# Last attention of a four-block network: second scores and value sums moved to the head of a step, next batch's preparation begun four steps sooner, first batch's preparation split over the engines

## The chip, the cores and the metric

One core of a Trainium2 chip runs the whole program. The metric is device time in microseconds (us) from start to end of one execution. The kernel before took 2774.77 us, the median of three executions (2765.41, 2774.77 and 2776.35).

Engines are named as the profile names them: PE is TensorE (PEld its weight loads), DVE is VectorE, ACT is ScalarE, POOL is GpSimd, SP issues DMAs. Each engine executes its own instructions in program order and waits on semaphores for the others.

## The reference

The network applies four blocks to `x` of shape (4, 512, 256): `x = x + layernorm(block(layernorm(x)))`. The blocks are a windowed attention, an attention with a mixture of experts, the attention changed here, and a second mixture of experts. The block that the change touches is:

```python
def _L1_attn_ref(x, ln_q_g, ln_q_b, Wq, bq, ln_kv_g, ln_kv_b, Wkv, bkv, ln_h_g, ln_h_b, Wo, bo):
    q = (layernorm(x, ln_q_g, ln_q_b) @ Wq + bq)      # 16 heads of 16
    kv = (layernorm(x, ln_kv_g, ln_kv_b) @ Wkv + bkv)
    ...
    q = apply_rotary(q, x)          # tables scaled by the norm of the row of x
    k = apply_rotary(k, x)
    qn = layernorm(q, ln_h_g, ln_h_b)                 # over each head's 16 values
    kn = layernorm(k, ln_h_g, ln_h_b)
    logits = jnp.einsum('bhqd,bhkd->bhqk', qn, kn) / jnp.sqrt(jnp.float32(HD))
    att = jax.nn.softmax(logits, axis=-1)
    a = jnp.einsum('bhqk,bhkd->bhqd', att, v)
    a = a.transpose(0, 2, 1, 3).reshape(b, c, d)
    return a @ Wo + bo
```

There are 4 batches of 512 rows. A batch is 4 tiles of 128 rows and has 16 heads, which is 8 pairs of heads.

## The kernel before

The stage is the function `attention2`. It is one software pipeline over steps `s`, and every engine runs the same loop over `s` with its own list of operations in each step. A batch has 32 steps: 4 groups of 8 steps, a group being two pairs of heads times four row tiles. Batch `b` has its scores in steps 32b to 32b+31. Below, `i` is the step within a batch, and "step 3 of a group" is `s % 8 == 3`.

Scores are computed twice. The first scores (`scores`, L1835, two matmuls into a pair of PSUM banks of `c_first`) serve only to find each row's maximum: `maximum` (L2080) on DVE. `c_first` has two such pairs, used in turn by everything that goes through it (list `pairs`), so that each use waits for the reader of the use before last. At the end of a group, `max_high` (L1972, ACT) and `max_low` (L2086, DVE) put the maxima into spare columns of the stacked q. The q of the group is turned again (`turn_q("again")`, L1821 on PE, copied by `copy_q`, L1966, on ACT). 14 steps after the first scores (`SECOND`) come the second scores, transposed (`scores_t`, L1848, two matmuls into the two banks of `c_second`). Then follow `exps` (L1980, two ACT operations), and two steps after that (`LAG`), once per two steps, the value sums (`values`, L1860, eight matmuls). Both banks of `c_second` are written in each step, so that `scores_t` of a step waits for both exponentials of the step before:

```python
if g >= 1:
    pe.wait_ge(s_ex, 2 * g)
```

In a step, PE's order before the change is: turn q again (step 3 of a group), first scores, turn q first (step 4; the q of the next group), turn keys, project, turn the outputs of a group (`turn_o`), the transposes `turn_a` and the output projection `out` of the batch before, then `scores_t`, and then `values` in odd steps. ACT's order is: `max_high` (step 0), copy q again (step 3), `exps`, copy q first, `copy_keys`, `root`, `high`, `copy_a`. DVE's is: `maximum`, `max_low` (step 1), `copy_o` (step 7), tables, `read_qk`, `cos_products`, `head_sums`, `centre`, `square_sums`, `inverse`, `read_v`, `divide`, `add_bias`. The function has no DMA in its loop.

The preparation of a batch runs during the scores of the batch before it; for batch 0 it runs ahead, in steps -32 to -1. For each of four tiles it is: `project("qk")` (L1802, PE), `read_qk` (L2033), `cos_products` (L2053) on DVE and `sin_products` (L2183) on POOL, `rotate` (L2189, POOL), `head_sums` (L2058), `centre` (L2063), `square` (L2194, POOL), `square_sums` (L2069), then for all four tiles together `root` (L1938, ACT) and `inverse` (L2075, DVE), then per tile `scale` (L2199), two `gains` (L2207) on POOL, `high` (L1950, four ACT copies), `low` (L2214, two POOL operations), `turn_keys` (L1812, PE) and `copy_keys` (L1959, ACT). `project("v")` has its own four steps, and its DVE reader is `read_v` (L2040). All projections, `turn_o`, `turn_a` and `out` share one bank (`c_x`, list `singles`), and each waits for the reader of the use before it. The steps come from `tile_at(s, first, apart)`: qk in i = 0, 3, 6, 9, v in 16 to 19, `root` and `inverse` in 17, `scale` in 18, 20, 22, 24, `high` in 20 to 26, `low` in 21 to 27, `turn_keys` and `copy_keys` in 23, 25, 27, 29.

## Time and profile before

| | us |
|---|---|
| median of three executions | 2774.77 |
| the profiled execution | 2782.3 |
| its span, first to last instruction | 2780.3 |
| the stage changed here, first projection to last bias | 1936 to 2364.6 |
| of it, preparation of batch 0 | 51.7 |
| of it, scores of the four batches and the tail | 377 |

The profile's page shows PE busy for 84% of the span, DVE for 59%, ACT for 46% and POOL for 49%, and a mean granted TensorE clock of 0.923 of full speed. The page's averages cover stages with different limits, so the changed stage is read alone. The tables by stretch give each engine's busy time between two points of time. The timeline gives single operations in order, with the idle time before each in brackets and what ended it.

### The profile page before, as it was taken

Reading aid. Unit: us, or ns where it says so; the run is one execution under the profiler, and the core shown is the slowest. Engines: PE = TensorE matmul, PEld = TensorE weight load, DVE = VectorE, ACT = ScalarE, POOL = GpSimd, SP = SyncE. Lnnn points to the kernel's source line nnn. Section 1 sums busy time; section 2 is a strip of 40 time slices with the busy share of each in tenths; the row PEclk is TensorE's granted clock in tenths of the full one; section 3 lists DMA queues with packets and bytes.
Section 4 is the critical chain, followed back from the end, with each engine's and each line's share of the span. In section 5 each row is a group of like instructions: output and inputs, shape, how many; then the busy total and the mean of one; then the engine's idle time right before and its main releaser. Section 6 shows DMA issues by size and latency. Waiting matters only on the chain. (4 is left out here: it accounts for less than half of the span.)

```text
span 2780.3 us, 41037 instructions
## 1 busy us (share of the span) xinstructions
PE 2342.3 (84%) x12100; PEld 1559.3 (56%) x12100; DVE 1649.0 (59%) x5313; ACT 1274.5 (46%) x3678; POOL 1358.1 (49%) x1301
## 2 busy tenths in 40 slices
PE   6999999994899999999998499963577887599991
PEld 5888888882455555555554456531333343466661
DVE  7667676665766766766774533327566753653334
ACT  3444444443556656656666244421166564143331
POOL 2444454441555555555554178862634310138885
PEclk9999999997899999999999599985799998699996
DMA  5000000002000000000001545550000000515554
GB/s 167 16 15 1 15 15 15 16 4 87 1 1 1 1 1 1 1 1 1 1 1 32 219 81 87 86 117 23 0 1 1 1 1 1 198 35 86 87 85 112
DMA packets 72818, 112.26 MB, mean 40 GB/s; under 512 B 11504, under 2 KB 59632, under 8 KB 72240
## 3 DMA queue, kind: packets, MB, share of 16 engines
q0 software_dynamic: 30336, 42.73, 9.3%
q1 hardware_dynamic: 38080, 63.15, 6.5%
q10 hardware_dynamic: 4224, 4.19, 0.4%
q8 instruction: 88, 1.44, 0.2%
q14 instruction: 90, 0.74, 0.1%
HBM read 80.69 MB, written 36.32 MB: 42 GB/s over the span
## 5 line engine op out<-in xcount | busy, mean ns | idle before, releaser
L1059 POOL TENSOR_TENSOR b_sm<-b_sm,b_rden 128x128 f32<-128x128 f32 (+3 forms) x512 | 355.7, 722 | 357.4 <-DVE b_rden L1012 357.4
L952 ACT ACTIVATE b_sm<-b_sm,b_mn 128x128 f32<-128x128 f32 (+3 forms) x512 | 285.1, 569 | 23.0 <-DVE b_mn L1004 22.0
L943 ACT ACTIVATE b_pt<-b_t 128x128 f32<-128x128 f32 (+3 forms) x512 | 196.1, 440 | 144.9 <-PE b_t L883 144.5
L1004 DVE CUSTOM_DVE_ANT_0 b_sm<-b_f,maskB 128x128 f32<-128x128 f32 (+3 forms) x512 | 233.5, 489 | 3.3 <-issue 2.2
L873 PE MATMUL b_f<-b_k,b_q 64*128 64x128 f32 (+3 forms) x1024 | 209.9, 486 | 29.1 <-DVE b_prod L993 14.7
L993 DVE SCALAR_TENSOR_TENSOR b_prod<-b_f,b_sin 32x512 f32<-32x512 f32 x320 | 219.9, 687 | 4.3
L1428 POOL DMA_INDIRECT XN<-rows,m_slots x158 | 158.1, 1001 | 94.0 <-issue 47.5
L2080 DVE TENSOR_REDUCE c_nm<-c_first 128x2 f32<-128x1024 f32 x128 | 155.1, 1219 | 82.2 <-PE c_first L1835 82.2
L1980 ACT ACTIVATE c_pt<-c_second 128x512 f32<-128x512 f32 x256 | 139.2, 598 | 123.8 <-PE c_second L1848 123.6
L883 PE MATMUL b_t<-ident,b_sm 128*128 128x128 f32 x1280 | 194.6, 283 | 0.9 <-ACT b_pt L943 0.8
L409 POOL TENSOR_TENSOR a_q<-a_prod 128x512 f32<-128x512 f32 x64 | 81.8, 1278 | 228.8 <-DVE a_prod L355 228.8
L883 PEld LDWEIGHTS b_t<-ident,b_sm 128*128 128x128 f32 x1280 | 143.4, 141 | 87.4 <-issue 60.5
L860 PE MATMUL b_f<-HT,b_w 128*128 128x512 f32 x320 | 154.6, 607 | 0.0
L897 PE MATMUL b_t<-b_pt,Y 128*64 128x512 f32 (+3 forms) x1024 | 151.9, 439 | 2.5 <-ACT b_pt L943 2.5
L1247 PE MATMUL m_p<-WM,Y 128*128 x316 | 151.5, 602 | 2.8 <-issue 2.8
L323 ACT ACTIVATE a_s<-a_s,a_nmx 128x192 f32<-128x192 f32 (+1 forms) x256 | 110.1, 431 | 87.6 <-DVE a_nmx L368 87.6
L1435 POOL DMA_INDIRECT acc<-Y,m_slots x79 | 125.4, 1587 | 32.0 <-issue 21.1
L1435 POOL DMA_INDIRECT acc<-m_plain,m_slots x79 | 125.4, 1588 | 30.8 <-issue 20.2
L908 PE MATMUL b_y<-b_wo,b_ot 128*128 128x256 f32 x512 | 134.9, 387 | 0.0
L897 PEld LDWEIGHTS b_t<-b_pt,Y 128*64 128x64 f32 x1024 | 68.4, 136 | 117.2 <-issue 78.1
L637 POOL TENSOR_TENSOR X<-X,Y 128x1024 f32<-128x1024 f32 x16 | 38.9, 2430 | 184.2 <-DVE Y L565 184.2
L873 PEld LDWEIGHTS b_f<-b_k,b_q 64*128 64x128 f32 x1024 | 79.0, 187 | 86.9 <-issue 62.3
(283 smaller groups left out, 5393.4 us busy)
## 6 DMA issues: line engine op xcount, KB each, us to landing
WM<-in_m_w_dram SPq DMA_DIRECT2D x4, 3072.0 KB, 17.5
WM<-in_m_w_dram SPq DMA_DIRECT2D x4, 2432.0 KB, 14.0
acc<-in_zeros_dram SPq DMA_DIRECT2D x3, 2176.0 KB, 16.2
n_part<-acc SPq DMA_DIRECT2D x12, 512.0 KB, 7.8
a_wa<-in_a_wa_dram SPq DMA_DIRECT2D x8, 512.0 KB, 4.5
b_w<-in_b_w_dram SPq DMA_DIRECT2D x1, 3072.0 KB, 9.9
XN<-rows,m_slots POOLq DMA_INDIRECT x158, 2.8
X<-in_x_dram SPq DMA_DIRECT2D x4, 512.0 KB, 5.7
```

What stands on the lines that cost most here:

```text
L860: x = pe.matmul(bank[:, :], w[:, k, pair, j, :], c.HT[:, k, b * SEQ:(b + 1) * SEQ], start=first, stop=last)
L873: pe.matmul(front_bank(("s", S, head))[:, 0:keys(t)], q_r[r, M % 3, t * P:(t + 1) * P], k_r[r, pg % 2, 0:keys(t)], start=True, stop=True). ...
L883: x = pe.transpose(bank[:, k * P:(k + 1) * P], sm[:, slot(S, head), k * P:(k + 1) * P], c.ident[:, :])
L897: x = pe.matmul(bank[r:r + B_HD, k * P:SEQ], v_s[:, b % 2, k, pair * P + r:pair * P + r + B_HD], pt[:, M % 2, head, k, k * P:SEQ], start=( ...
L943: act.activation(pt[:, M % 2, head, 0:t + 1, t * P:(t + 1) * P], back_bank(("t", S, head))[:, 0:keys(t)].rearrange("p (k n) -> p k n", n=P ...
L952: act.activation(sm[:, s, 0:keys(t)], sm[:, s, 0:keys(t)], ACT.Exp, scale=-1.0, bias=mn[:, s:s + 1], accum_out=den[:, s:s + 1]).then_inc(s ...
L993: x = dve.scalar_tensor_tensor(to[dst, 1, :], bank[src, :], scale, sin[src, :], ALU.mult, ALU.mult)
L1004: dve.tensor_tensor_reduce(sm[:, s, 0:keys(t)], front_bank(("s", S, head))[:, 0:keys(t)], mask[:, SEQ - keys(t):SEQ], 1.0, -3 * NEG, ALU.a ...
L1059: pool.tensor_tensor(sm[:, s, 0:keys(t)], sm[:, s, 0:keys(t)], rden[:, s:s + 1].to_broadcast([P, keys(t)]), ALU.mult).then_inc(s_pn, 1)
L1428: pool.indirect_dma_start(out=xg[:, b % RING, :], out_offset=None, in_=rows_dram[:, :], in_offset=IOA(ap=slots[:, b:b + 1], axis=0)).then_ ...
L1435: pool.indirect_dma_start(out=acc_dram[b % 2][:, :], out_offset=IOA(ap=slots[:, b:b + 1], axis=0), in_=ys[:, b % 4, :], in_offset=None, co ...
L2080: dve.tensor_reduce(nm[:, t, 2 * j:2 * j + 2], two_banks(("max", f)), AX.X, ALU.max, negate=True).then_inc(s_nm, 1)
```

## The change

It does four things, all in `attention2`.

1. In PE's loop, `scores_t` and `values` move from the end of a step to its head, ahead of "turn q again" and of the first scores. DVE's and ACT's orders are not changed by this.
2. The preparation of batches 1 to 3 starts four steps sooner: qk in i = -4, -1, 2, 5 (28 and 31 of the batch before that), products one step and rotate two steps after each, `root` in 13, `inverse` in 14, `scale` in 14 to 20, `low` in 18 to 24, keys in 20, 22, 24, 26, v in 18 to 21. `high` is split into `high_q` (two copies) and `high_k` (two copies, a step later), with a semaphore each.
3. "Turn q first" moves from step 4 to step 5 of a group, `turn_o` and `divide` from 29 to 25 steps after the group's first step, `turn_a` from 55 and 56 to 54 and 55. The loop has 2 steps fewer at its end and 4 more at its start.
4. Batch 0's preparation gets its own schedule (`EARLY`). `root` and `inverse` run for one tile at a time, so that `scale` begins in i = 5 and not 18. `sin_products` and `scale` go from POOL to DVE, `square` from POOL to ACT. Keys are turned in i = 10, 13, 16, 19.

```diff
@@ -1677,19 +1677,22 @@
     NP = PER_BATCH * BATCH
     TURN, SECOND, LAG = 3, 14, 2
     QUADS = 2
-    FIRST_STEP, LAST_STEP = -PER_BATCH, NP - PER_BATCH + 62
+    FIRST_STEP, LAST_STEP = -PER_BATCH - 4, NP - PER_BATCH + 60

     def turned_again(s):
         return s // GROUP - 1 if s % GROUP == TURN and 0 <= s // GROUP - 1 < GROUPS_ALL else None

     def turned_first(s):
-        return s // GROUP + 1 if s % GROUP == 4 and 0 <= s // GROUP + 1 < GROUPS_ALL else None
-
-    def tile_at(s, first, apart):
-
-        b, i = s // PER_BATCH + 1, s % PER_BATCH - first
-        t = i // apart
-        return b * TB + t if b < BATCH and i % apart == 0 and 0 <= t < TB else None
+        return s // GROUP + 1 if s % GROUP == 5 and 0 <= s // GROUP + 1 < GROUPS_ALL else None
+
+    def tile_at(s, what):
+
+        for b in range(BATCH):
+            first, apart = (EARLY if b == 0 else LATER)[what]
+            i = s - PER_BATCH * (b - 1) - first
+            if i >= 0 and i % apart == 0 and i // apart < TB:
+                return b * TB + i // apart
+        return None

...

-    KEYS_AT, PROJ_AT, V_AT, O_AT, A_AT, OUT_AT = 23, 0, 16, 29, 55, 58
+    O_AT, A_AT, OUT_AT = 25, 54, 58
+    LATER = {"qk": (-4, 3), "products": (-3, 3), "rotate": (-2, 3), "sums": (0, 3), "centre": (1, 3), "square": (2, 3),
+             "square_sums": (3, 3), "scale": (14, 2), "shift": (15, 2), "high_q": (16, 2), "high_k": (17, 2), "low": (18, 2),
+             "keys": (20, 2), "v": (18, 1)}
+    EARLY = {**LATER, "scale": (5, 3), "shift": (6, 3), "high_q": (7, 3), "high_k": (7, 3), "low": (8, 3), "keys": (10, 3)}
...
                 def turn_keys(n):
-                    pe.wait_ge(s_hi, n + 1)
+                    pe.wait_ge(s_hik, n + 1)
                     pe.wait_ge(s_lo, n + 1)
                     pair_free(("keys", n))
                     to = two_banks(("keys", n))
...
                 for s in range(FIRST_STEP, LAST_STEP):
+                    g, m = s - SECOND, s - SECOND - LAG
+                    if 0 <= g < NP:
+                        scores_t(g)
+                    if 0 <= m < NP and m % 2 == 1:
+                        values(m // 2)
                     if turned_again(s) is not None:
                         pe.wait_ge(s_nl, turned_again(s) + 1)
                         turn_q("again", turned_again(s), s_tr2)
...
                     if turned_first(s) is not None:
                         grp = turned_first(s)
                         if grp % 4 == 0:
-                            pe.wait_ge(s_hi, grp + 4)
+                            pe.wait_ge(s_hiq, grp + 4)
                             pe.wait_ge(s_lo, grp + 4)
                             if grp >= 8:
                                 pe.wait_ge(s_clear, grp // 4 - 1)
                         turn_q("first", grp, s_trq)
-                    if tile_at(s, KEYS_AT, 2) is not None:
-                        turn_keys(tile_at(s, KEYS_AT, 2))
-                    if tile_at(s, PROJ_AT, 3) is not None:
-                        project("qk", tile_at(s, PROJ_AT, 3))
-                    if tile_at(s, V_AT, 1) is not None:
-                        project("v", tile_at(s, V_AT, 1))
+                    if tile_at(s, "keys") is not None:
+                        turn_keys(tile_at(s, "keys"))
+                    if tile_at(s, "qk") is not None:
+                        project("qk", tile_at(s, "qk"))
+                    if tile_at(s, "v") is not None:
+                        project("v", tile_at(s, "v"))
                     if group_at(s, O_AT) is not None:
                         turn_o(group_at(s, O_AT))
...
-                    g = s - SECOND
-                    if 0 <= g < NP:
-                        scores_t(g)
-                    m = g - LAG
-                    if 0 <= m < NP and m % 2 == 1:
-                        values(m // 2)
...
+                def root(n, tiles):
+
+                    act.wait_ge(s_ssq, n + tiles)
+                    at = slice(n % TB, n % TB + tiles)
+                    act.activation(std[:, at, :], ssq[:, at, :], ACT.Sqrt, bias=c.eps[:, :], scale=1.0 / C_HD).then_inc(s_std, 1)
+
+                def square(n):
+                    act.wait_ge(s_cen, n + 1)
+                    act.wait_ge(s_ssq, n)
+                    act.activation(sq[:, :], qk[:, n % TB, :], ACT.Square).then_inc(s_sq, 1)
+
+                def high_q(n):
                     b, t = n // TB, n % TB
+                    act.wait_ge(s_n, n + 1)
+                    if b >= 2 and t == 0:
+                        act.wait_ge(s_tr2, (b - 1) * 4)
+                    for place in (0, 1):
+                        x = act.activation(stack_q[b % 2][:, t, :, place * C_HD:(place + 1) * C_HD].bitcast(F32R),
+                                           heads(qk[:, t, 0:DIM]), ACT.Copy)
+                    x.then_inc(s_hiq, 1)
+
+                def high_k(n):
                     act.wait_ge(s_n, n + 1)
                     if n >= 2:
                         act.wait_ge(s_trk, n - 1)
-                    if b >= 2 and t == 0:
...
+                    for place in (0, 2):
+                        x = act.activation(stack_k[:, n % 2, :, place * C_HD:(place + 1) * C_HD].bitcast(F32R),
+                                           heads(qk[:, n % TB, DIM:W2]), ACT.Copy)
+                    x.then_inc(s_hik, 1)
...
-                    if tile_at(s, KEYS_AT, 2) is not None:
-                        copy_keys(tile_at(s, KEYS_AT, 2))
-                    if i == 17 and b < BATCH:
-                        root(b)
-                    if tile_at(s, 20, 2) is not None:
-                        high(tile_at(s, 20, 2))
+                    if tile_at(s, "keys") is not None:
+                        copy_keys(tile_at(s, "keys"))
+                    if i == 13 and 0 < b < BATCH:
+                        root(b * TB, TB)
+                    if tile_at(s, "square") is not None and tile_at(s, "square") < TB:
+                        square(tile_at(s, "square"))
+                    if tile_at(s, "square_sums") is not None and tile_at(s, "square_sums") < TB:
+                        root(tile_at(s, "square_sums"), 1)
+                    if tile_at(s, "high_q") is not None:
+                        high_q(tile_at(s, "high_q"))
+                    if tile_at(s, "high_k") is not None:
+                        high_k(tile_at(s, "high_k"))
...
+                def inverse(n, tiles):
+
+                    b, at = n // TB, slice(n % TB, n % TB + tiles)
+                    dve.wait_ge(s_std, n + 1 if b == 0 else TB + b)
                     if b > 0:
                         dve.wait_ge(s_scaled, b * TB)
-                    dve.reciprocal(rstd[:, :, :], std[:, :, :]).then_inc(s_rs, 1)
+                    dve.reciprocal(rstd[:, at, :], std[:, at, :]).then_inc(s_rs, 1)
...
+                def scale(n):
+                    dve.wait_ge(s_rs, n + 1)
...
+                def sin_products(n):
+                    dve.wait_ge(s_r, n)
...
-                    if i == 0 and b < BATCH:
-                        tables_of(b)
-                    if tile_at(s, PROJ_AT, 3) is not None:
-                        read_qk(tile_at(s, PROJ_AT, 3))
-                    if tile_at(s, 1, 3) is not None:
-                        cos_products(tile_at(s, 1, 3))
-                    if tile_at(s, 4, 3) is not None:
-                        head_sums(tile_at(s, 4, 3))
-                    if tile_at(s, 5, 3) is not None:
-                        centre(tile_at(s, 5, 3))
-                    if tile_at(s, 7, 3) is not None:
-                        square_sums(tile_at(s, 7, 3))
-                    if i == 17 and b < BATCH:
-                        inverse(b)
-                    if tile_at(s, V_AT, 1) is not None:
-                        read_v(tile_at(s, V_AT, 1))
+                    if i == PER_BATCH - 4 and b + 1 < BATCH:
+                        tables_of(b + 1)
+                    if tile_at(s, "qk") is not None:
+                        read_qk(tile_at(s, "qk"))
+                    if tile_at(s, "products") is not None:
+                        cos_products(tile_at(s, "products"))
+                        if tile_at(s, "products") < TB:
+                            sin_products(tile_at(s, "products"))
+                    if tile_at(s, "sums") is not None:
+                        head_sums(tile_at(s, "sums"))
+                    if tile_at(s, "centre") is not None:
+                        centre(tile_at(s, "centre"))
+                    if tile_at(s, "square_sums") is not None:
+                        square_sums(tile_at(s, "square_sums"))
+                    if i == 14 and 0 < b < BATCH:
+                        inverse(b * TB, TB)
+                    if tile_at(s, "scale") is not None and tile_at(s, "scale") < TB:
+                        inverse(tile_at(s, "scale"), 1)
+                        scale(tile_at(s, "scale"))
+                    if tile_at(s, "v") is not None:
+                        read_v(tile_at(s, "v"))
...
-                    pool.wait_ge(s_rs, n // TB + 1)
+                    pool.wait_ge(s_rs, TB + n // TB)
...
+                    pool.wait_ge(s_hiq, n + 1)
+                    pool.wait_ge(s_hik, n + 1)
...
+                    if tile_at(s, "products") is not None and tile_at(s, "products") >= TB:
+                        sin_products(tile_at(s, "products"))
+                    if tile_at(s, "rotate") is not None:
+                        rotate(tile_at(s, "rotate"))
+                    if tile_at(s, "square") is not None and tile_at(s, "square") >= TB:
+                        square(tile_at(s, "square"))
+                    if tile_at(s, "scale") is not None:
+                        if tile_at(s, "scale") >= TB:
+                            scale(tile_at(s, "scale"))
+                        gains(tile_at(s, "scale"), 0)
+                    if tile_at(s, "shift") is not None:
+                        gains(tile_at(s, "shift"), 1)
+                    if tile_at(s, "low") is not None:
+                        low(tile_at(s, "low"))
```

## Rows read from the trace of the kernel before

**Rows 1.** Busy us (x instructions) by stretch: PE, PEld, DVE, ACT, POOL; PEclk; DMA share.
```profile
1936.00:1987.70 51.70, 27.57 (x74) 15.17 (x74) 20.17 (x33) 10.75 (x22) 36.46 (x36) 0.60 0.00 0
1987.70:2019.10 31.40, 21.17 (x76) 9.79 (x76) 29.43 (x41) 5.67 (x7) 13.92 (x15) 0.84 0.00 1
2019.10:2067.20 48.10, 36.53 (x206) 18.43 (x206) 25.47 (x30) 32.35 (x61) 20.96 (x21) 0.93 0.00 1
2161.50:2254.70 93.20, 74.88 (x424) 36.17 (x424) 60.85 (x84) 54.73 (x102) 34.94 (x36) 0.98 0.00 1
2254.70:2317.80 63.10, 55.39 (x352) 25.08 (x352) 43.93 (x50) 41.21 (x76) 0.00 (x0) 1.00 0.00 1
2317.80:2345.60 27.80, 20.18 (x103) 6.35 (x102) 4.13 (x8) 17.07 (x32) 0.00 (x0) 0.78 0.00 1
```

**Rows 2.** Timeline: start, us, engine, line, [idle before]; steps 96 to 104, no preparation.
```profile
2256.15 0.51 PE L1835 MATMUL c_first<-c_kt,c_qt 64*128 64x512 f32 x2
...
2258.51 1.06 PE L1860 MATMUL c_pv<-c_pt,c_v 128*32 128x512 f32 x8
...
2259.84 0.42 PE L1848 MATMUL c_second<-c_qt,c_kt 64*128 64x512 f32 x2
...
2260.19 1.10 PE L1821 MATMUL c_first<-ident,XN 128*128 128x128 f32 x8
2260.30 1.08 ACT L1980 ACTIVATE c_pt<-c_second 128x512 f32<-128x512 f32 x2 [0.59 <-PE c_second L1848]
...
2261.32 0.51 PE L1835 MATMUL c_first<-c_kt,c_qt 64*128 64x512 f32 x2
2261.32 1.03 ACT L1966 ACTIVATE c_qt<-c_first 128x1024 fp32r<-128x1024 f32 x1
...
2261.87 1.22 DVE L2080 TENSOR_REDUCE c_nm<-c_first 128x2 f32<-128x1024 f32 x1 [0.60 <-PE c_first L1835]
...
2262.24 1.08 ACT L1980 ACTIVATE c_pt<-c_second 128x512 f32<-128x512 f32 x2
...
2271.20 0.51 PE L1835 MATMUL c_first<-c_kt,c_qt 64*128 64x512 f32 x2
2271.29 0.23 ACT L1972 ACTIVATE c_stack_q<-c_nm 128x16 fp32r<-128x16 f32 x1
```

**Rows 3.** Timeline, PE: first scores of steps 64, 72 and 88 (batch 2).
```profile
2163.03 0.50 PE L1835 MATMUL c_first<-c_kt,c_qt 64*128 64x512 f32 x2
...
2184.60 0.49 PE L1835 MATMUL c_first<-c_kt,c_qt 64*128 64x512 f32 x2
...
2227.32 0.49 PE L1835 MATMUL c_first<-c_kt,c_qt 64*128 64x512 f32 x2
```

**Rows 4.** PE's groups in batch 2 (busy, mean ns, idle before); a table load on ACT.
```profile
L1802 PE MATMUL c_x<-c_wqkv,HT 128*128 128x512 f32 (+1 forms) x32 | 12.5, 512 | 4.1 <-DVE c_v L2040 3.6 <-DVE c_a_t L2108 0.5
...
L1812 PE MATMUL c_first<-ident,c_stack_k 128*128 128x128 f32 x32 | 5.2, 315 | 3.9 <-ACT c_qt L1966 3.9
...
2210.71 1.28 ACT L1980 ACT_TABLE_LOAD   x1
```

**Rows 5.** Timeline of batch 0's preparation.
```profile
1945.94 0.69 DVE L2063 SCALAR_TENSOR_TENSOR c_qk<-c_hsum,c_qk 128x512 f32<-128x512 f32 x1
...
1951.02 1.44 DVE L2063 SCALAR_TENSOR_TENSOR c_qk<-c_hsum,c_qk 128x512 f32<-128x512 f32 x1
...
1964.26 2.61 POOL L2207 TENSOR_TENSOR c_qk<-c_qk,c_gq 128x512 f32<-128x512 f32 x2
1964.54 2.08 PE L1802 MATMUL c_x<-c_wqkv,HT 128*128 128x256 f32 x4 [0.52 <-DVE c_v L2040]
...
1967.54 0.71 ACT L1950 ACTIVATE c_stack_k<-c_qk 128x256 fp32r<-128x256 f32 x2
...
1982.19 1.94 PE L1812 MATMUL c_first<-ident,c_stack_k 128*128 128x128 f32 x8 [3.09 <-ACT c_stack_k L1950]
...
1982.85 0.73 POOL L2214 TENSOR_TENSOR c_stack_k<-c_qk,c_stack_k 128x256 fp32r<-128x256 f32 x1
```

More of the change, by code:

```diff
@@ L1708, in attention2 @@
             pairs.append(("first", turned_first(s)))
-        if tile_at(s, KEYS_AT, 2) is not None:
-            pairs.append(("keys", tile_at(s, KEYS_AT, 2)))
-        if tile_at(s, PROJ_AT, 3) is not None:
-            singles.append(("qk", tile_at(s, PROJ_AT, 3)))
-        if tile_at(s, V_AT, 1) is not None:
-            singles.append(("v", tile_at(s, V_AT, 1)))
+        if tile_at(s, "keys") is not None:
+            pairs.append(("keys", tile_at(s, "keys")))
+        if tile_at(s, "qk") is not None:
+            singles.append(("qk", tile_at(s, "qk")))
+        if tile_at(s, "v") is not None:
+            singles.append(("v", tile_at(s, "v")))
         if group_at(s, O_AT) is not None:
@@ L1761, in attention2 @@
         s_sq, s_ssq, s_std, s_rs = sem("square"), sem("square_sum"), sem("std"), sem("rstd")
-        s_scaled, s_p, s_n, s_hi, s_lo = sem("scaled"), sem("times_gain"), sem("normed"), sem("high"), sem("low")
+        s_scaled, s_p, s_n, s_lo = sem("scaled"), sem("times_gain"), sem("normed"), sem("low")
+        s_hiq, s_hik = sem("high_q"), sem("high_k")
         s_trk, s_ke, s_trq, s_qe = sem("keys_turned"), sem("keys_copied"), sem("q_turned"), sem("q_copied")
```

40 lines of the change are left out of this document (11 added, 29 removed).

## The prediction

> **What bounds the kernel now.** I read the page for its own time first: the profiled execution took 2782.3 us, 2.0 more than its span and 7.5 more than the median of 2774.8, so I work out a difference on the trace and add it to the median. Only `attention2` changes, and no DMA moves in it [rows 1]. The table by stretch shows four regimes. In batch 0's preparation (51.7 us) POOL is busy for 36.5 us and PE idles at a granted clock of 0.60. From the first scores to step 15 (31.4 us) DVE is full: 29.4 busy. In batch 2, as in batch 1, PE is busy for 74.9 of 93.2 us, and no engine is full. In batch 3, without preparation, a group of 8 steps takes 15.05 us (first scores at 2256.15 and 2271.20 [rows 2]), and PE's 55.4 of 63.1 us is not what holds it. The timeline shows what does: a loop through PE and ACT. The exponentials take 1.08 us, the next second scores wait for both of them, and the exponentials after that start about 0.46 us after their matmuls do (2259.84 and 2260.30), so that a step takes at least 1.08 + 0.46 and some 0.1 for the handing over, 1.7 us [rows 2].
>
> **The head of the step.** PE's order repeats from step to step, so moving `scores_t` (T) and `values` (V) to the head only rotates it: T comes one place earlier against the first scores (S), and V lies ahead of "turn q again" (A) and not behind it. What counts is what lies between the end of one pair of exponentials and the start of the next. Durations: T and S hold PE for 0.43 each, V 1.0, A or "turn q first" (F) 1.02, a copy of q 1.03 and an exponential pair 1.08 [rows 2].
> - Step 3 (A). Before, A runs during the exponentials of step 2, and T runs during A's copy, which is why the pairs at 2260.30 and 2262.24 are 1.94 apart although a copy lies between them [rows 2]. ACT's order still has the copy ahead of the exponentials. After, A stands behind T and V, and T behind the exponentials of step 2: 1.08 + 0.06 + 0.43 + 1.0 + 1.02 + 0.11 + 1.03 = 4.7 us apart, 2.8 more.
> - Step 0. `max_high` is ahead of `exps` on ACT and waits for the maximum of step 7. S now follows V: 1.42 for T and V, 0.55 to DVE, 1.22 for the maximum, 0.3 for the copy, so the exponentials of step 0 start 3.5 us after T of step 7 and 3.0 after its exponentials, not 1.7: 1.3 more. Before, `max_high` at 2271.29 waited for nothing [rows 2].
> - Steps 4 and 5 (F). F at step 5 lies after T, V and S, with its copy ahead of the next exponentials: 3.5 us. At step 4 it made one interval of about 2.7 and one of 1.9; now the others are 1.7. Together 0.3 more or less, taken as 0.
> - `turn_o` (0.6) moves into an odd step, beside V: T + V + S + 0.6 = 2.45 against 1.7, 0.8 more.
>
> A group without preparation goes from eight intervals of 15.05 to 3.0 + 1.7 + 2.45 + 4.7 + 1.7 + 1.7 + 3.5 + 1.7 = 20.4. The same addition for the order before gives 15.6, 0.5 too much, so I take +5.0 for a group. Batch 3 has four: +20, less 2.4 since the two output projections there no longer lie beside V and A on PE: +17.5. The tail has one step 0, one step 3 and one `turn_o` more, at a clock of 0.78 [rows 1]: +4.5.
>
> **Batches 1 and 2.** Here PE is 80% busy, and the waits above are filled with preparation. I added up a batch in the same way, group by group, from 19.6 us (20.4 less the walk's 4% excess): group 1 with projections in steps 2 and 5 and one left over from step 31, +4.5 = 24.1; group 2 with ACT's root, 1.28 + 0.4 + 1.28, +3 = 22.6; group 3 with v and keys, +3.3 = 22.9; group 4 with keys, one output projection beside nothing else, and the next projection, +4.2 = 23.8; in all 93.4. Before, the first group took 21.6, the next two 42.7 and the last 28.8, which is 93.1 (first scores at 2163.03, 2184.60, 2227.32 and 2256.15 [rows 2, 3]). So the gain is where the keys were: 28.8 becomes about 24, because keys no longer share steps 27 and 29 with A and F. PE waited 3.9 us a batch for a copy of q ahead of `turn_keys`, and 3.6 for `read_v`, which was queued on DVE behind `inverse` [rows 4]. It is given back in groups 1 and 2 through steps 0 and 3. I take +0.5 for each batch, +1 in all. The bounds are -7.5 (those two PE waits gone, nothing given back) and +7.
>
> **Batch 0's scores.** Steps 0 to 15 are DVE's [rows 1]. Two of batch 1's tiles are read and one is multiplied before step 0, and T of a step now precedes S of that step: -2.3. ACT loads a table once where it did three times between step 14 and step 18, as the roots of batch 1 now come before the first exponentials: two loads of 1.28 and a stall behind them [rows 4]. With the quieter group of keys this makes 43.1 for the 48.1 us [rows 1]: -5.0.
>
> By the Trainium skill (ScalarE: Activation LUTs, "What ACT_TABLE_LOAD costs") a switch of tables costs about 2.66 us with a drain, not the load of 1.28 alone. By it, batch 0 would gain some 2.8 us more; no row shows a drain.
>
> **Batch 0's preparation.** Splitting root and inverse lets `scale` of tile 0 finish at about 1954, nine us sooner than before. From there POOL has two gains (2.6) and two `low` (1.45) a tile [rows 5]. But there is a loop: in i = 10, 13 and 16 ACT copies the keys of a tile first and does `high` of the next tile behind that, so `high` waits for `turn_keys` of the tile before. One turn of that loop is low 1.45, `turn_keys` 1.94 at the low clock, copy 1.03, high 1.43, and 0.25 of handing over: 6.1 us a tile, against 5.05 of POOL alone before. From `low(0)` at 1962.5 three turns end `low(3)` at 1980.8, where it was 1983.6 [rows 5]. Then PE still has, in order, keys 3 (1.94), v of tiles 1 to 3 (2.08 each at the low clock [rows 5], 1.13 at the high one, plus 0.5 for `read_v`), the projection of tile 4 (1.98), F (1.1) and the projection of tile 5 (1.98) ahead of the first scores: 11 to 14 us. Before, it was 4.1. The first scores come at 1990 to 1994.5 where they came at 1987.7: I take +4.5, with bounds of -1.5 (all at the high clock, POOL's pace) and +7.
>
> **The sum.** +4.5 - 2.3 - 5.0 + 1 + 17.5 + 4.5 = +20.2. On the median: 2774.8 + 20.2 = 2795.
>
> **The rivals.**
> 1. The waits of steps 0 and 3 cost little, since ACT has slack (41.2 busy of 63.1 in batch 3 [rows 1]), and the earlier preparation gives what it can: -7.5 in each of batches 1 and 2, -7.3 in batch 0, -1.5 in the preparation, 0 in batch 3: -24, 2751. Against it: ACT's slack is idle time inside the loop and not beside it [rows 2]. Chance 0.1.
> 2. Both hold by half: batch 3 and the tail +11, batches 1 and 2 together -5, batch 0 -7, the preparation +2: +1, 2776. Chance 0.3.
> 3. Slower than forecast: with PE idling longer in batch 3, its granted clock falls as in the tail (0.78 against 1.00 [rows 1]). This decides if PE's busy share of 0.88 there falls to the tail's 0.73; my sum gives 55.4 of 80.6, 0.69. T, V, A and S of batch 3 then take up to twice their time: in the loop that is 8 x 0.1, A and V 2.0, F 1.0 and so on, about 4 a group: +36, 2811. Chance 0.15.
> 4. DVE and POOL hold each other up in batch 0's preparation. `centre` took 1.44 us at one place, beside POOL's `rotate`, and 0.69 at another [rows 5]. If all two-input operations of tiles 2 and 3 on DVE are stretched so, (0.75 + 1.1 + 0.7) x 2, the first scores come 5 us later still: 2800. Chance 0.05.
>
> The Trainium skill (SBUF — State Buffer, "SBUF: two separate sides") calls the port pair that DVE and GpSimd share an exclusive lock, whose loser waits for the whole instruction; by that rule rival 4 holds, and moving work from POOL to DVE gains nothing there.
>
> **How the numbers follow.** The forecast case has 0.4 by itself, between 2785 and 2805. The range that should hold 8 in 10 takes in rivals 2 to 4 and the bounds of the preparation and of the middle batches: 2768 to 2818; rival 1 and a worse clock are left out. A difference of 0.5%, 14 us, is about what a measurement of this kernel can tell from none. Faster by that is rival 1 with a little of rival 2: 0.12. Within it is most of rival 2 and the low end of the forecast: 0.30. Slower is the rest: 0.58.
>
> **What would show each step.** In the profile after: exponentials 4.7 us apart around A in batch 3, with ACT idle until `c_first` L1821; ACT idle before `max_high`, released by DVE `c_nm`; a period of about 20 us a group in batch 3 at PE busy of 0.7; the waits of `turn_keys` on `c_qt` gone and the fourth group of batches 1 and 2 near 24; two table loads fewer on ACT in batch 0; the first scores 54 to 58 us after the first projection. I am wrong if batch 3 still takes 63 us, or if PE's V and A fit into the exponentials' shadow.

## The result

The changed kernel takes 2840.22 us (median of 4, 2830.73 to 2847.46) against 2772.21 for the kernel before: a ratio of 1.0236, 95% interval 1.0207 to 1.0265. That is +68 us where +20.2 was forecast, and outside the range. The profiled execution took 2844.9 us, its span is 2843.1.

Between the two profiled executions (2782.3 and 2844.9 us) the stage went from 427.7 to 493.0 us, counted from the first projection to the end of the last output projection, and the rest of the program was 2.7 shorter. I cut the stage at the second scores of steps 15, 31, 63, 95 and 127, which are the same work in every kernel of this study, and use these stretches throughout, as the rest of the program varies by several us from run to run. Each row of stretches comes from one execution.

| stretch | before | after | measured | forecast |
|---|---|---|---|---|
| preparation of batch 0 | 51.5 | 57.1 | +5.5 | +4.5 |
| first scores to step 15 | 31.4 | 36.3 | +4.9 | -2.3 |
| 15 to 31 | 48.1 | 45.6 | -2.5 | -5.0 |
| batch 1, 31 to 63 | 94.4 | 104.7 | +10.3 | +0.5 |
| batch 2, 63 to 95 | 93.1 | 103.2 | +10.1 | +0.5 |
| batch 3, 95 to 127 | 64.0 | 89.3 | +25.3 | +17.5 |
| tail, 127 to the end | 45.1 | 56.7 | +11.6 | +4.5 |

The table by stretch of the kernel after (columns as in [rows 1]) has the same stretches; the last line ends at step 141.

```profile
1937.20:1994.30 57.10, 29.50 (x80) 15.71 (x80) 27.88 (x53) 13.59 (x29) 23.48 (x22) 0.67 0.00 0
1994.30:2030.60 36.30, 19.26 (x65) 9.96 (x64) 30.91 (x38) 5.96 (x8) 14.16 (x16) 0.72 0.00 0
2030.60:2076.20 45.60, 39.52 (x208) 18.91 (x208) 24.52 (x31) 29.95 (x58) 21.93 (x23) 0.85 0.00 1
2076.20:2181.00 104.80, 83.44 (x426) 39.06 (x426) 61.57 (x84) 55.11 (x101) 34.92 (x37) 0.85 0.00 1
2181.00:2284.20 103.20, 81.22 (x420) 37.70 (x420) 59.35 (x77) 55.10 (x101) 32.32 (x34) 0.85 0.00 1
2284.20:2373.60 89.40, 65.91 (x354) 28.75 (x354) 44.07 (x50) 42.64 (x77) 0.00 (x0) 0.85 0.00 0
2373.60:2411.00 37.40, 25.96 (x102) 8.20 (x102) 4.82 (x9) 16.22 (x30) 0.00 (x0) 0.57 0.00 1
```

DVE and ACT are busy in batches 1 to 3 for what they were before. PE is busy for 81.2 us in batch 2 where [rows 1] has 74.9, and for 65.9 in batch 3 where it had 55.4, though it executes the same matmuls: the granted clock is 0.85 of full speed in all three batches, where it was 0.96, 0.98 and 1.00. The forecast had reckoned with the waits alone.

The waits are there, as forecast. The timeline of batch 3 after, a group at the full clock:

```profile
2334.21 0.23 ACT L1992 ACTIVATE c_stack_q<-c_nm 128x16 fp32r<-128x16 f32 x1 [1.60 <-DVE c_nm L2122]
2334.33 1.07 ACT L2000 ACTIVATE c_pt<-c_second 128x512 f32<-128x512 f32 x2
...
2335.45 0.50 PE L1856 MATMUL c_second<-c_qt,c_kt 64*128 64x512 f32 x2 [2.06 <-ACT c_pt L2000]
...
2338.44 1.08 ACT L2000 ACTIVATE c_pt<-c_second 128x512 f32<-128x512 f32 x2 [1.36 <-PE c_second L1856]
...
2341.01 1.09 PE L1829 MATMUL c_first<-ident,c_stack_q 128*128 128x128 f32 x8
...
2342.14 1.02 ACT L1986 ACTIVATE c_qt<-c_first 128x1024 fp32r<-128x1024 f32 x1 [2.61 <-PE c_first L1829]
...
2343.06 1.08 ACT L2000 ACTIVATE c_pt<-c_second 128x512 f32<-128x512 f32 x2
...
2344.19 0.50 PE L1856 MATMUL c_second<-c_qt,c_kt 64*128 64x512 f32 x2 [1.66 <-ACT c_pt L2000]
```

`max_high` waits 1.60 us for the maximum of step 7, and the exponentials of step 0 stand behind it. "Turn q again" (A) stands behind T and V, its copy waits 2.61, and the exponentials at 2338.44 and 2343.06 are 4.62 apart (4.7 forecast, 1.94 before [rows 2]). PE idles 2.06 and 1.66 us for them. One turn from A to A is 19.94 us here (20.4 forecast). But the turn before it, with the same operations, is 24.62 long. The table by stretch, from A to A:

```profile
2296.45:2321.07 24.62, 18.06 (x88) 7.56 (x85) 10.89 (x12) 10.62 (x19) 0.00 (x0) 0.71 0.00 1
2321.07:2341.01 19.94, 13.04 (x89) 5.53 (x85) 10.89 (x12) 10.62 (x19) 0.00 (x0) 1.00 0.00 0
```

DVE and ACT do the same to a hundredth; PE takes 5.0 us more and the turn 4.7. So in this turn nearly all that PE loses at the low clock is lost to the whole.

### The profile page after: what moved, and what is told of

The parts are those of the page before. It is cut to its first block and busy times, and to the rows that moved or that the text cites. A ratio compares the mean times of both kernels' runs of the same rounds, so it can differ in the third digit from the quotient of the medians.

```text
span 2843.1 us, 41054 instructions
## 1 busy us (share of the span) xinstructions
PE 2372.7 (83%) x12100; PEld 1569.2 (55%) x12100; DVE 1658.3 (58%) x5328; ACT 1276.5 (45%) x3683; POOL 1343.9 (47%) x1285
## 5 line engine op out<-in xcount | busy, mean ns | idle before, releaser
L952 ACT ACTIVATE b_sm<-b_sm,b_mn 128x128 f32<-128x128 f32 (+3 forms) x512 | 285.0, 569 | 22.9 <-DVE b_mn L1004 22.0
L1856 PE MATMUL c_second<-c_qt,c_kt 64*128 64x512 f32 x256 | 74.1, 575 | 81.4 <-ACT c_pt L2000 81.2
## 6 DMA issues: line engine op xcount, KB each, us to landing
WM<-in_m_w_dram SPq DMA_DIRECT2D x4, 3072.0 KB, 17.5
```

Source lines behind the costliest of these rows:

```text
L952: act.activation(sm[:, s, 0:keys(t)], sm[:, s, 0:keys(t)], ACT.Exp, scale=-1.0, bias=mn[:, s:s + 1], accum_out=den[:, s:s + 1]).then_inc(s ...
```

## The experiments

Times in us; stretches as above, the last two columns the tail and the whole stage. The ratio is to the kernel before on the same chip, with its 95% interval. The kernel before had medians of 2776.9 to 2780.8 on the chips of the experiments, so kernels of different rows are compared by the ratio or by the stage and not by the median alone.

| kernel | median | ratio | prep. | to 15 | to 31 | b. 1 | b. 2 | b. 3 | tail | stage |
|---|---|---|---|---|---|---|---|---|---|---|
| before | 2772.2 | 1 | 51.5 | 31.4 | 48.1 | 94.4 | 93.1 | 64.0 | 45.1 | 427.7 |
| after | 2840.2 | 1.0236 [1.0207, 1.0265] | 57.1 | 36.3 | 45.6 | 104.7 | 103.2 | 89.3 | 56.7 | 493.0 |
| e1_head_only | 2787.2 | 1.0043 [1.0017, 1.0068] | 51.5 | 31.4 | 45.3 | 90.9 | 87.8 | 80.0 | 43.9 | 430.8 |
| e2_no_head | 2789.1 | 1.0052 [1.0032, 1.0072] | 54.7 | 36.0 | 48.2 | 101.0 | 99.8 | 63.6 | 42.1 | 445.4 |
| e3_again_first | 2783.0 | 1.0025 [0.9999, 1.0051] | 54.7 | 36.0 | 42.5 | 94.7 | 94.5 | 75.6 | 39.8 | 437.7 |
| e4_scores_twice | 2829.9 | 1.0207 [1.0156, 1.0257] | 54.6 | 36.0 | 43.3 | 105.2 | 102.2 | 89.0 | 47.7 | 478.0 |
| e5_again_tv_scores | 2766.7 | 0.9945 [0.9926, 0.9964] | 52.3 | 31.4 | 45.5 | 86.1 | 85.9 | 73.3 | 43.9 | 418.3 |
| e6_max_high_late | 2753.0 | 0.9900 [0.9878, 0.9921] | 52.4 | 30.9 | 43.8 | 84.7 | 83.3 | 67.6 | 39.4 | 402.1 |
| e7_high_ahead | 2823.0 | 1.0156 [1.0125, 1.0186] | 51.8 | 37.1 | 44.4 | 102.9 | 103.5 | 90.5 | 47.7 | 477.8 |
| e8_early_only | 2781.7 | 1.0002 [0.9985, 1.0020] | 54.1 | 31.4 | 54.3 | 94.8 | 95.8 | 64.1 | 39.0 | 433.5 |
| e9_both_orders | 2780.4 | 1.0008 [0.9986, 1.0029] | 54.7 | 36.0 | 42.3 | 91.0 | 88.5 | 70.0 | 41.3 | 423.9 |
| e10_first_in_4 | 2766.9 | 0.9972 [0.9947, 0.9998] | 57.2 | 34.7 | 41.6 | 89.6 | 88.7 | 68.0 | 41.4 | 421.2 |
| e11_both_high_ahead | 2774.7 | 0.9994 [0.9974, 1.0013] | 51.8 | 37.1 | 41.9 | 89.6 | 88.5 | 70.0 | 41.4 | 420.3 |
| e12_late_early | 2743.8 | 0.9886 [0.9860, 0.9912] | 48.4 | 31.4 | 42.4 | 85.6 | 83.3 | 67.5 | 41.2 | 399.8 |
| e13_filled | 2814.9 | 1.0145 [1.0105, 1.0185] | 57.3 | 36.0 | 45.6 | 101.2 | 98.2 | 82.4 | 47.5 | 468.0 |
| e14_again_filled | 2791.9 | 1.0054 [1.0027, 1.0081] | 54.7 | 36.0 | 42.5 | 96.3 | 95.1 | 75.3 | 41.5 | 441.3 |

The preparation of one and the same code took 54.7 or 57.1 us, at a granted clock of 0.72 or 0.67: a difference of 2.5 us there says nothing about a kernel.

**The two halves of the change.** e1 is the kernel before with only the head:

```diff
                 for s in range(FIRST_STEP, LAST_STEP):
+                    g, m = s - SECOND, s - SECOND - LAG
+                    if 0 <= g < NP:
+                        scores_t(g)
+                    if 0 <= m < NP and m % 2 == 1:
+                        values(m // 2)
                     if turned_again(s) is not None:
...
-                    g = s - SECOND
-                    ...
```

> The kernel before with the second scores and value sums at the head of a step, and nothing else changed. Theory W (the order at the head makes new waits on ACT at steps 0 and 3 of a group, and the idle PE then loses its clock): 3.0 + 1.7 + 1.85 + 4.7 + 1.7 + 2.5 + 2.45 + 1.7 = 19.6 us for a group of batch 3 at the high clock instead of 15.05, up to 25 with part of it at the low one; in all +40 to +60 us on the 2772 of before, 2812 to 2832. Theory P (the moved preparation and batch 0's own schedule cost most of the 68 us): at most +20, under 2795, and batch 3 near 64 us.

e2 is the kernel after with these lines back at the end of the step.

> The changed kernel with the second scores and value sums back at the end of a step, and the rest of the change kept. Theory W: batch 3 back near 64 us and a clock near 1.00 from step 32 to 127, batches 1 and 2 at 93 or a little under, the preparation of batch 0 still 5 us longer: 2765 to 2782. Theory P: the loss stays, over 2815.

Both missed, and in the same way: batch 3 came as expected (e1 80.0, e2 63.6), the middle batches did not. The head alone makes them 3.5 and 5.3 us shorter, the rest of the change alone 6.6 and 6.7 longer, the two together 10.3 and 10.1 longer. Over the stage e1 adds 3.1 us and e2 17.7, and both together 65.3: 44.5 us belong to neither half alone, but to the two meeting.

**One swap.** e3 is the kernel after with A ahead of T and V at the head of the step, so that A runs during the exponentials before it.

```diff
                 for s in range(FIRST_STEP, LAST_STEP):
+                    if turned_again(s) is not None:
+                        pe.wait_ge(s_nl, turned_again(s) + 1)
+                        turn_q("again", turned_again(s), s_tr2)
                     g, m = s - SECOND, s - SECOND - LAG
```

> The changed kernel with one swap: in step 3 of a group, turning q again is put ahead of the second scores and value sums. Theory W: the pairs of exponentials around it are about 2 us apart and not 4.7, so 2.7 us less in each of 16 groups, 43 us, and some of the clock's loss besides: 2785 to 2797. The wait of max_high in step 0 stays. If the clock were lost for another reason, under 15 us would come back: over 2825.

The median fell by 57 us (ratio 1.0236 to 1.0025), the stage by 55.3: more than the 44.5 that neither half explains. The same swap on the old preparation (e5 below against e1) takes 12.5 off the stage. So A's place behind T and V costs 12.5 us there and 55.3 with the moved preparation, and this difference of 42.8 is nearly all of the 44.5.

**The clock.** e4 repeats the first scores of even steps.

```diff
-                    for half in range(2):
+                    for half in (0, 1) * (2 - f % 2):
```

> The changed kernel with each pair of first-score matmuls of an even step executed twice into the same banks (64 pairs more, 0.43 us each, 27 us of work for PE that computes nothing new). Theory W says that the part of the loss beyond the walk is the granted clock, which falls where PE idles: with PE busier the clock from step 31 to 127 rises from 0.85 to 0.95 or more, and the time falls by 5 to 20 us, to 2820 to 2835. If the clock is not what PE's idle time costs, the added work leaves the time equal or makes it 5 to 27 us longer.

The time came as expected, the clock did not: it stayed near 0.85 in batches 1 to 3, these kept their length, and the gain of 15.0 us in the stage lies ahead of and behind them. With the clock unmoved, the lower time does not bear out the theory. The copies were spread evenly, not where PE waits. e13 puts them there, from batch 1 on:

```diff
-                    for half in range(2):
+                    for half in (0, 1) * (1 + ((4, 0, 2, 3, 1, 0, 2, 0)[f % GROUP] if f >= PER_BATCH else 0)):
```

> The changed kernel with copies of the first scores of the same step (same values into the same banks, which do no useful work) from batch 1 on: four more in step 0 of a group, two in step 2, three in step 3, one in step 4, two in step 6, each just ahead of a place where PE waits for the exponentials (2.06, 0.95, 1.66, 0.82 and some 1.3 us in batch 3): 0.4 us each, 4.8 us a group, so that PE works through those waits and still comes to its second scores in time. No wait and no order is changed. Theory K (the low granted clock after these waits costs the time: within the changed kernel the same work between two "turn q again" took 24.6 us with low stretches and 19.9 without): the granted clock of batch 3 goes from 0.85 to 0.97 or more, batch 3 takes 79 to 83 us and not 89.3, the middle batches 94 to 99 and not 104.7 and 103.2, the steps from 127 to 141 some 34 and not 37.5, and the kernel 2808 to 2822. Rival (the order's waits alone set the time, and the low clock lies in their shadow): batch 3 stays at 87 to 90 us whatever the clock, the middle batches get longer by the copies that lie beside preparation, 104 to 109, 2838 to 2852.

> The same copies in e3_again_first ("turn q again" ahead of second scores and value sums, 2783, mostly at full clock): what the copies cost by themselves. There the waits ahead of the second scores are shorter in steps 3 and 4. Theory K: batch 3 at full clock, 71 to 77 us for 75.6, the middle batches within 3 us of e3's 94.7 and 94.5, so 2777 to 2790. Rival (the copies are in the way as such): 2 to 4 us more in each of the three batches, 2790 to 2800.

Batches 1 to 3 and the steps to 141 of e13:

```profile
2066.20:2167.30 101.10, 88.29 (x522) 45.23 (x522) 60.07 (x83) 55.29 (x101) 34.90 (x37) 0.93 0.00 1
2167.30:2265.50 98.20, 84.25 (x518) 43.53 (x518) 58.85 (x78) 55.29 (x101) 32.42 (x34) 0.97 0.00 1
2265.50:2347.80 82.30, 68.38 (x448) 33.92 (x448) 44.46 (x51) 42.65 (x77) 0.00 (x0) 0.98 0.00 1
2347.80:2380.20 32.40, 20.74 (x104) 6.66 (x104) 4.85 (x9) 16.22 (x30) 0.00 (x0) 0.79 0.00 1
```

PE executes 94 more matmuls in batch 3 than after (448 for 354), is busy for 2.5 us more and ends 7 us sooner, at a clock of 0.98 and not 0.85. The waits are the same ones, only filled: in the group from 2285.35 the exponentials still let PE wait 1.14 and 0.97 us behind 1.30 and 1.19 us of scores. The kernel is 25 us faster with 288 matmuls more. The middle batches gained 3.5 and 5.0, less than expected in batch 1, where the clock came to 0.93 only. The control e14 puts the same copies into e3, whose clock is mostly full without them, and gets 1.6, 0.6 and -0.3 us longer in the three batches: the copies gain nothing by themselves. Its median is 1.9 above the expected range, at the low end of its rival's, but the rival's 2 to 4 us a batch are not there; its stage is 3.6 above e3's. The kernels with PE's order of after and without these copies take 297.2 (after), 296.4 (e4) and 296.9 us (e7) in batches 1 to 3, e13 281.8. So some 15 us in the three batches were the low clock and not the waits. Another 9.2 lie in the tail, where the clock went from 0.57 to 0.79 up to step 141; but e4 and e7, whose tails have 0.75 there without these copies, are as short (47.7), so that the copies are not shown to be the cause of that part.

**Orders that suit the loop.** e5 is the kernel before with PE's order A, T, V, S; e6 is e5 with `max_high` behind the exponentials on ACT:

```diff
-                    if s % GROUP == 0 and 0 <= s // GROUP - 1 < GROUPS_ALL:
-                        max_high(s // GROUP - 1)
                     if turned_again(s) is not None:
...
                         exps(s - SECOND)
+                    if s % GROUP == 0 and 0 <= s // GROUP - 1 < GROUPS_ALL:
+                        max_high(s // GROUP - 1)
```

> The kernel before with PE's step in the order: turn q again, second scores, value sums, first scores, and the rest as before. The run with the head alone showed the middle batches 3.5 and 5.4 us shorter and batch 3 with its tail 17 us longer. If the A wait (turn q again behind the value sums) is the larger part of those 17, batch 3 comes down from 20 to about 17 us a group, the second group of batches 1 and 2 from 20.3 to 18.6 or less, and the whole to 2757 to 2770. If the gain in the middle hung on A coming late, the whole stays at 2775 to 2790.

> The run before it with max_high put behind the exponentials on ACT. If the wait of max_high for the maximum of step 7 costs 1.3 us a group as worked out (3.0 us between pairs of exponentials and not 1.7), 16 groups give 10 to 20 us: 2742 to 2757. If DVE's max_low, which waits for max_high and has the next maximum queued behind it, is then late, the gain is under 5 us.

Both medians are in their ranges, and both kernels are faster than before, by 0.5 and 1.0%. In e5 the second groups of batches 1 and 2 took 18.9 and 20.4 us, not 18.6 or less. ACT's timeline of e6 around step 0 of a group:

```profile
2250.40 1.09 ACT L1979 ACTIVATE c_pt<-c_second 128x512 f32<-128x512 f32 x2 [0.59 <-PE c_second L1848]
2251.41 0.23 ACT L1971 ACTIVATE c_stack_q<-c_nm 128x16 fp32r<-128x16 f32 x1
2252.07 1.09 ACT L1979 ACTIVATE c_pt<-c_second 128x512 f32<-128x512 f32 x2 [0.43 <-PE c_second L1848]
```

`max_high` waits for nothing, and the exponentials are 1.67 apart. The loop of step 0 is confirmed: taking it off saved 16.2 us of the stage and 14 of the median. In batch 3 a group is 16.2 us, still 1.2 more than before, but the middle batches are 10 us shorter at clocks of 0.98 and 1.00.

**The moved preparation.** e9 has e6's two orders on top of the kernel after, e10 has e9 with "turn q first" (F) in step 4 again.

> The changed kernel with "turn q again" ahead of second scores and value sums (as in e3_again_first, 2783) and `max_high` behind the exponentials (as in e6_max_high_late, 2753): the moved preparation on the order that was fastest. Theory C (the moved preparation costs time by itself: root and inverse in step 13 beside "turn q again" at 11, keys and v together in 18 to 26, two things on PE in step 5): the late `max_high` takes off what it took off before, 13 to 16 us, and the kernel stays at 2766 to 2774, with 89 to 93 us in each middle batch against 84.7 and 83.3 of e6, 36 from the first scores to step 15, and 67 to 69 in batch 3. Rival (only the orders cost, and with both of them right the moved preparation is harmless): 2748 to 2758, middle batches of 82 to 86.

> As e9_both_orders, with "turn q first" back in step 4 of a group. In step 5 it stands on PE with a projection (i = 5, tile 3 of the next batch) and, in batch 0's scores, behind it. Theory C1 (this meeting in step 5 makes the 4.6 us between the first scores and step 15, and part of the longer middle batches): 32 to 34 instead of 36 in that stretch, 1 to 3 us less in each middle batch, in all 4 to 9 us less than e9. Rival (what is late there is DVE, with the reads, products and sums of three tiles ahead of the maxima): 36 stays, and the kernel is within 2 us of e9.

e9's median missed its range by 6 us, and batch 3 its own by 1; the other stretches hit within half a us. Against e3, whose order it shares but for `max_high`, its stage is 13.8 us shorter, as expected, its median only 2.5. The stage is 21.8 us longer than e6's, 11.5 of it in batches 1 and 2. The moved preparation costs on the best order too. e10's median is 13.5 us less than e9's, where 4 to 9 were expected, but its stage only 2.7, or 5.2 without the preparation of batch 0, whose 57.2 for 54.7 says nothing: 1.3 of them before step 15, where 2 to 4 were expected, and 1.4 and -0.2 in batches 1 and 2. F beside a projection in step 5 is a part of it only. Where e2's schedule loses in the middle batches its profile shows in part: in the second group ACT's `root` with two table loads of 1.28 now stands between the exponentials of steps 45 and 46, and the group takes 21.9 us for 18.6; the third group, with keys and v, takes 29.3 for 25.6.

**Batch 0's preparation.** e7 is the kernel after with `high_q` and `high_k` ahead of `copy_keys` on ACT, e8 the kernel before with only batch 0's preparation changed, e11 is e9 with e7's swap, e12 is e6 with e8's schedule and e7's swap.

```diff
-                    if tile_at(s, "keys") is not None:
-                        copy_keys(tile_at(s, "keys"))
...
                     if tile_at(s, "high_k") is not None:
                         high_k(tile_at(s, "high_k"))
+                    if tile_at(s, "keys") is not None:
+                        copy_keys(tile_at(s, "keys"))
```

> The changed kernel with ACT's copies of the prepared q and k ahead of the copy of the keys in the same step. If the loop through turn_keys and its copy sets the pace of batch 0's preparation (5.9 us a tile in the trace), the pace falls to 5.1 to 5.3, and the preparation from 55 to 57 us to 53 to 55; the whole 2 to 4 us shorter, 2836. If POOL alone sets it, nothing changes.

> The kernel before with batch 0's own schedule alone (preparation from four steps sooner, split over the engines); batches 1 to 3 prepared as before, all orders as before. The preparation takes 51 to 53 us where the whole change has 55 to 57, since no tile of batch 1 is projected ahead of the first scores; the steps from there are as before, 31.4 us to step 15. In all 0 to +3 us. If the split by itself made the scores behind it slower, as in the changed kernel, step 15 would come 36 us after the first scores.

> As e9_both_orders, with ACT's `high_q` and `high_k` ahead of `copy_keys` in a step (as in e7_high_ahead, where batch 0's preparation took 51.8 us for 57.1 and the whole 17 us less). Theory L (the loop keys, copy, high is only in batch 0's preparation): the preparation takes 50 to 52.5 us for e9's 54.5 to 57, the other stretches stay within 1 us each, 3 to 5 us less than e9. Rival (it also frees the middle batches, where keys of one tile and `high_q` of the next share steps 20 and 22): 1 to 3 us less in each of them too, 6 to 10 less than e9.

> e6_max_high_late (before, with PE's order A, T, V, S and a late `max_high`: 2753) with only batch 0's preparation changed, as in e8_early_only, and `high_q` and `high_k` ahead of `copy_keys`. Theory L (the loop is what held the split preparation back): the preparation takes 49 to 51.5 us where e6 took 52.4 and e8 54.1, the scores of batches 0 to 3 are as in e6 (30.9, 43.8, 84.7, 83.3, 67.6, each within 2 us), 2750 to 2754. Rival (moving POOL's work of batch 0 to DVE and ACT delays tile 4 of the next batch and lowers the granted clock behind it, as e8's 54.3 us at 0.78 for 48.1 at 0.93 from step 15 to 31 suggest): the preparation is as short, but 2755 to 2762 in all.

PE turning keys in the preparation, first after, then e7:

```profile
1964.84 1.94 PE L1820 MATMUL c_first<-ident,c_stack_k 128*128 128x128 f32 x8 [13.19 <-POOL c_stack_k L2262]
...
1970.75 1.94 PE L1820 MATMUL c_first<-ident,c_stack_k 128*128 128x128 f32 x8 [3.97 <-POOL c_stack_k L2262]
...
1976.62 1.94 PE L1820 MATMUL c_first<-ident,c_stack_k 128*128 128x128 f32 x8 [3.92 <-issue]
```

```profile
1960.11 1.94 PE L1820 MATMUL c_first<-ident,c_stack_k 128*128 128x128 f32 x8 [2.21 <-POOL c_stack_k L2262]
...
1964.83 1.94 PE L1820 MATMUL c_first<-ident,c_stack_k 128*128 128x128 f32 x8 [2.78 <-issue]
...
1968.97 1.84 PE L1820 MATMUL c_first<-ident,c_stack_k 128*128 128x128 f32 x8 [0.49 <-issue]
```

A turn takes 5.9 us after (6.1 forecast), and 4.7 and 4.1 with the swap. The preparation takes 51.8 us in e7 and e11, for the 57.1 and 54.7 that the code without the swap takes; from e8 to e12, which also have different orders, it is 5.7 shorter. In e7 the pace and the preparation came in below what was expected (5.1 to 5.3, and 53 to 55). For its median 2836 was expected and it was 2823: of the 15.2 us of its stage 9.0 lie in the tail, and e4 has them too, so they are not the swap's. e8 missed its preparation by 1 us, without the swap, and lost 6.2 us between steps 15 and 31 at a granted clock of 0.78; e12, with the good orders, did not, and that place of e8 stays unexplained. e11 came nearly as expected, with 3.6 us less than e9 in the stage. In e12 the preparation is 0.6 us shorter than expected and the other stretches are e6's within 2; its median, 2743.8, is 6 us below the expected 2750 to 2754, which its stage does not explain.

e12 has the shortest stage, 27.9 us less than before. Its ratio and e6's (0.9886 and 0.9900) can't be told apart; both beat the kernel before by about 1%.

## Why the prediction failed

- **Step 3 and step 0 of a group: right.** 4.62 us between exponentials for 4.7, 1.60 us ahead of `max_high`, 19.94 for 20.4 a group at the full clock. With the waits filled (e13), batch 3 is 18.4 us longer than before, where +17.5 was forecast.
- **The clock: the step that failed.** The sum priced every wait with PE's operations at full speed, in the middle batches too, and put nothing for the clock. Rival 3 had it, but with a chance of 0.15, in batch 3 and the tail only, and tied it to PE's share falling to the tail's 0.73. After, PE is busy for 0.74 of batch 3 and for 0.79 of batch 2 (81.2 of 103.2), and the clock is 0.85 in both. PE's busy time rose by 7.2, 6.3, 10.5 and 5.8 us in batches 1 to 3 and the steps to 141. I had treated the middle batches as filled with preparation. The stage is 45.1 us above the forecast. Of these, 15.4 are the clock in batches 1 to 3, as e13 shows; some 7 are in the tail, at 0.57 to step 141; 2.5 are in steps 15 to 31, at 0.85; 7.2 are in the first scores to step 15; 10.9 are left in the middle batches, and 2 in the preparation and batch 3.
- **The middle batches: the second step that failed.** Of +20.4, e13 gives back 8.5, against a forecast of +1. The fourth group was right (23.7 and 22.6 us for 28.6 and 28.8, "about 24" forecast). The first three take 26.1, 26.0 and 29.0 us in batch 1 (24.1, 22.6 and 22.9 forecast), at clocks of 0.93, 0.83 and 0.68; the third of batch 2, at 0.90, took 24.0. By these two third groups 0.22 of clock is worth 5.0 us. An estimate at that rate, 23 us for the whole of it, puts batch 1's groups at 24.5, 22.1, 21.7 and 23.7, in all 92.0, where the walk had 93.4. By the same rate e13's 101.2 and 98.2, at 0.93 and 0.97, become 95 each, its copies included. So the walk may have been right at a full clock, or 2 us short; that is argued only. One interval can be read. In step 45 `root` stands on ACT behind F's copy, and the exponentials on both sides of it are 8.4 us apart. The walk has 3.5 for F and 2.96 for `root` with its loads, 6.5, and 6.5 is what e9 takes there at a full clock (step 77). Here V and F run at the low clock. PE waits 4.57 us, the longest of its waits in the four batches' scores:

```profile
2118.76 1.08 ACT L2000 ACTIVATE c_pt<-c_second 128x512 f32<-128x512 f32 x2 [0.89 <-PE c_second L1856]
...
2124.14 1.28 ACT L1947 ACT_TABLE_LOAD   x1
...
2127.15 1.09 ACT L2000 ACTIVATE c_pt<-c_second 128x512 f32<-128x512 f32 x2
...
2128.29 0.80 PE L1856 MATMUL c_second<-c_qt,c_kt 64*128 64x512 f32 x2 [4.57 <-ACT c_pt L2000]
```

- **First scores to step 15: sign wrong.** -2.3 forecast, +4.9 measured. The stretch is 36.0 to 37.1 us in every kernel with the moved preparation and F in step 5, 34.7 with F in step 4 (e10), and 30.9 to 31.4 in every kernel without the moved preparation. I had counted the work that leaves this stretch, and not the projections of batch 1 that now stand on PE behind F, at a low clock (0.72 for the whole stretch): DVE, the full engine, waits for one of them.

```profile
2008.19 2.86 PE L1810 MATMUL c_x<-c_wqkv,HT 128*128 128x512 f32 x4
...
2011.08 0.69 DVE L2059 TENSOR_TENSOR c_qk<-c_x,c_bias 128x512 f32<-128x512 f32 x1 [2.98 <-PE c_x L1810]
```

  DVE's 2.98 us behind F and the projection, and 1.5 us more of work (30.91 for 29.43), make 4.5; before, no wait of DVE in this stretch was longer than 1.06. In e10, with F in step 4, that wait was still 2.08, behind the projection alone, so F is the smaller part.
- **15 to 31.** The two table loads fewer were there. -2.5 at a clock of 0.85, and -4.8 in e4, with the same order and 0.93, so -5.0 was about right but for the clock. That the moved preparation gains it is not shown: e9 and e11 have -5.8 and -6.2, but e6 and e12, without it, -4.3 and -5.7. The Trainium skill (ScalarE: Activation LUTs, "What ACT_TABLE_LOAD costs") has 2.66 us for a switch. Here the exponentials start 0.02 us behind the load, and the root in front of it ends 0.01 us ahead of it; this trace has no drain there, and 1.28 is the price.

```profile
2027.78 0.39 ACT L1947 ACTIVATE c_std<-c_ssq,eps 128x128 f32<-128x128 f32 x1
...
2028.18 1.28 ACT L2000 ACT_TABLE_LOAD   x1
...
2029.48 1.09 ACT L2000 ACTIVATE c_pt<-c_second 128x512 f32<-128x512 f32 x2
```

- **Preparation of batch 0: right within 1.3 us**, +5.5 (or +3.2 in the kernels at 0.72) for +4.5, by the loop through keys and `high`. Rival 4's stretching is there in places, but the 5 us that it would add are not: beside POOL's two gains, the two cosine products took 1.82 us (0.75 at 2074.31 in the same trace) and the first sine product 1.48 (0.41 for the second), 1.07 longer each.

```profile
1954.59 1.82 DVE L2079 TENSOR_TENSOR c_products<-c_qk,c_mcos 128x256 f32<-128x256 f32 x2
1954.75 2.78 POOL L2254 TENSOR_TENSOR c_qk<-c_qk,c_gq 128x512 f32<-128x512 f32 x2 [2.21 <-DVE c_qk L2107]
1956.33 1.48 DVE L2116 TENSOR_TENSOR c_products<-c_qk,c_mneg 128x256 f32<-128x256 f32 x1
1957.73 0.41 DVE L2116 TENSOR_TENSOR c_products<-c_qk,c_msin 128x256 f32<-128x256 f32 x1
```

  The Trainium skill (SBUF — State Buffer, "SBUF: two separate sides") has the loser of that port pair wait for the whole instruction; one gains instruction is 1.27 us, and by that rule, the trace agrees: neither product was held up for more than one.
- **The tail.** +11.6 for +4.5: the clock fell from 0.77 to 0.57 up to step 141. At 0.79 (e13) the tail has +2.4, at 0.75 (e4, e7) +2.6, so the order's own part was nearer 2.5 than 4.5.

**Open** is how the moved preparation's cost in the middle batches divides, 5 to 6 us each on the best order (e9 against e6). It is not the clock alone: the first two groups of batch 2 run at 1.00 in both kernels and take 23.5 and 20.3 us in e9, 20.5 and 18.9 in e6. In the first, the exponentials of steps 66 and 67 are 5.4 us apart for 3.2, those of steps 69 and 70 5.1 for 2.0. Open is also why the clock falls with some waits of 1 to 2 us and not with others: e3 keeps 0.93 to 0.95 with PE busy for 0.77 to 0.80 of a batch, not much more than after.

## What to carry over

Where two engines hand work to each other once a step, write down which operation of each step lies between the end of one engine's turn and the start of its next: here an operation put behind such a wait cost its whole duration plus that of its reader, and ahead of it little or nothing. One swap on PE was worth 57 us with the moved preparation (12.5 of the stage with the old one), and one on ACT another 14. And a wait on PE has a second price: work out the stretches again with the matmuls at the lower clock before calling any stretch with idle PE safe.

## What the hardware showed

In the kernel after, TensorE's granted clock fell from its upper level (2.4 GHz) to its lower one (1.2 GHz), for several us at a time, in batches 1 to 3, where PE was busy for 0.80, 0.79 and 0.74 of the time; in batch 3 no wait was longer than 2.06 us, in batches 1 and 2 the longest was 4.57. The mean over the batches was 0.85. Ahead of the T at 2345.86, which takes 0.80 us and not 0.50, PE had idled 0.95, 1.66 and 0.82 us at its last three second scores. With 12 copies of a first score in these waits in each group the clock of batch 3 was 0.98, and batches 1 to 3, with more work, were 15.4 us shorter.
